# A decoder layer in split float32: cross output in two passes a pair of heads, first columns turned by VectorE and transfers

## What is computed

```python
x = x + self_attn(layernorm(x))    # blocks of 128 rows, causal softmax, one head of 512
x = x + cross_attn(layernorm(x), ctx)   # 16 heads of 32, 64 keys, silu(masked scores), no softmax
x = x + ffn(layernorm(x))          # 512 -> 2048, gelu, -> 512
```

## Time and profile before

| | us |
|---|---|
| median of 3 runs (lowest, highest) | 1262.47 (1262.35, 1262.99) |
| the profiled execution's own time | 1262.69 |
| its span | 1260.6 |
| TensorE busy | 1248.7 |
| VectorE / ScalarE / GpSimd busy | 664.6 / 487.1 / 243.5 |
| a middle step | 63.17 |

### The profile page before, as it was taken

The page is one execution under the profiler, slowest core; times in us unless marked ns, Lnnn a source line. Parts: engine busy times, 40 slices in busy tenths (PEclk is TensorE's granted clock), DMA queues, the critical chain, the costliest instruction groups (busy, mean ns, idle before and its releaser), DMA issues.

```text
span 1260.6 us, 15609 instructions
## 1 busy us (share of the span) xinstructions
PE 1248.7 (99%) x5784; PEld 1040.2 (83%) x5784; DVE 664.6 (53%) x1210; ACT 487.1 (39%) x888; POOL 243.5 (19%) x226
## 2 busy tenths in 40 slices
PE   9989999999999999999999999999999999999998
PEld 7878888888888888878888888888888888888887
DVE  7476858585858585856733333434424333434211
ACT  7246454555555555554322232222222322223221
POOL 2303232323232323258402001001001010010000
PEclk9999999999999999999999999999999999999999
DMA  8210202020202020316110020020100100100000
GB/s 296 89 63 13 76 14 75 13 76 12 75 12 75 12 75 12 125 57 211 50 67 1 1 67 1 1 67 0 57 9 0 67 0 0 67 0 0 34 1 34
DMA packets 40486, 60.04 MB, mean 48 GB/s; under 512 B 4224, under 2 KB 14464, under 8 KB 40448
## 3 DMA queue, kind: packets, MB, share of 16 engines
q1 hardware_dynamic: 40448, 59.53, 14.2%
HBM read 41.17 MB, written 18.35 MB: 47 GB/s over the span
## 4 chain that ended last, share of the span: by engine, by line
PE 55%; DVE 0%; issue 0%; DVEq 0%
PE bank L50 18%; PE bank L51 18%; PE bank L52 18%; DVE resid L1191 0%; DVEq L1190 0%
## 5 line engine op out<-in xcount | busy, mean ns | idle before, releaser
L1181 DVE TENSOR_TENSOR hid_lo<-gelu_out,hid_hi 128x512 fp32r<-128x512 f32 x128 | 98.5, 770 | 404.1 <-ACT gelu_out L1145 404.0
L50 PE MATMUL bank<-zT,w_parts 128*128 128x512 f32 x768 | 299.1, 389 | 3.4 <-DVE zT L155 1.8
L52 PE MATMUL bank<-zT,w_parts 128*128 128x512 f32 x768 | 298.8, 389 | 0.0
L51 PE MATMUL bank<-zT,w_parts 128*128 128x512 f32 x768 | 298.8, 389 | 0.0
L1141 ACT ACTIVATE hid_hi<-bank,small 128x512 fp32r<-128x512 f32 x128 | 88.3, 690 | 498.4 <-PE bank L52 498.4
L50 PE MATMUL bank<-w2p_hi,hid_lo 128*128 128x512 f32 x512 | 199.2, 389 | 0.0
L51 PE MATMUL bank<-w2p_lo,hid_hi 128*128 128x512 f32 x512 | 199.2, 389 | 0.0
L52 PE MATMUL bank<-w2p_hi,hid_hi 128*128 128x512 f32 x512 | 199.2, 389 | 0.0
L50 PEld LDWEIGHTS bank<-zT,w_parts 128*128 128x128 f32 x768 | 144.1, 188 | 34.1 <-issue 2.3
L51 PEld LDWEIGHTS bank<-zT,w_parts 128*128 128x128 f32 x768 | 144.3, 188 | 30.0
L52 PEld LDWEIGHTS bank<-zT,w_parts 128*128 128x128 f32 x768 | 144.1, 188 | 30.0
(11 more groups left out here) (142 smaller groups left out, 1805.5 us busy)
## 6 DMA issues: line engine op xcount, KB each, us to landing
x_in<-in_x SPq DMA_DIRECT2D x32, 256.0 KB, 3.1
x_dram<-resid SPq DMA_DIRECT2D x32, 256.0 KB, 2.1
w_raw<-in_w SPq DMA_DIRECT2D x32, 256.0 KB, 3.2
resid<-x_dram SPq DMA_DIRECT2D x32, 256.0 KB, 3.8
out_dram<-resid SPq DMA_DIRECT2D x32, 256.0 KB, 2.1
resid<-in_wqkvT SPq DMA_DIRECT2D x12, 256.0 KB, 4.7
mask_i<-in_mask SPq DMA_DIRECT2D x16, 128.0 KB, 2.6
values_now<-values_dram SPq DMA_DIRECT2D x8, 256.0 KB, 2.7
```

The costliest lines, as they stand in the source:

```text
L50: pe.matmul(out_ap, lhs[1], rhs[0], start=start, stop=False)
L51: pe.matmul(out_ap, lhs[0], rhs[1], start=False, stop=False)
L52: return pe.matmul(out_ap, lhs[0], rhs[0], start=False, stop=stop)
L1181: dve.tensor_tensor(hid[1][:, c % 4, :], gelu_out[:, c % 2, :], f(hid[0][:, c % 4, :]), ALU.subtract).then_inc(hid_lo, 1)
```

## The change

1. vb is one array: a pair's 64 output columns hold the values' high parts, the other 64 their low parts. A pair gets a bank of its own and two passes (with the low and the high part of attn). Half of the rows of the bank are then the high values' share and the other half the low values' share of the same output. ScalarE copies the high share of each of the chunk's two banks (64 rows each) into qo's high part, and the other half of the rows, crossed to the partner's partitions, into `rest`; VectorE subtracts (two operations of 64 rows) into o_diff; GpSimd adds o_diff and rest into qo's low part. All banks are laid out anew, and waits for them change (`outputs_out`).
2. z1 of tile a + 1 is made a step ahead: x is loaded a second time into `ahead` (four of the weight buffers), its statistics and normed rows follow a tile earlier, VectorE transposes 32 x 32 squares (4 operations of 128 x 512) into the same buffers, and 16 transfers put the squares in their places in z1_cols. ScalarE and VectorE split z1_cols instead of banks. TensorE's transposes of z1 go, but for tile 0.
3. Orders are moved: GpSimd adds the bias to x_in at the start of the step; the statistics of blocks 2 and 3 come after z2's low parts; the output shares run by halves of chunks; in the last step z3's transposes of blocks 2 and 3 stand between shares 0 and 1.

The diff, cut:

```diff
-OUT_BANK = (3, 4, 5, 1)
-BLOCK_BANK = (6, 7, 0, 2)
+PROB_BANK = 5
+SCORE_BANK = (4, 5, 6, 7, 1, 2, 7, 0)
+OUT_BANK = (7, 0, 3, 4, 0, 5, 1, 2)
+BLOCK_BANK = (3, 4, 6, 7)
+TURN_BANK = (0, 5, 1, 2)
...
+            vb = sb("vb", [P, PAIRS, P], fp32r)
+            o_diff = sb("o_diff", [P, 2, TILE])
+            o_rest = raws[:, NB:NB + 2, :]
...
-                        tuple(v[r, :, :].rearrange("p (m o) n -> p m o n", o=2)[:, :, h // 2, cols(h, HEAD_DIM)]
-                              for v in vb),
+                        tuple(vb[r, :, :].rearrange("p (m o) n -> p m o n", o=2)[:, :, h // 2, cols(at_cols, HEAD_DIM)]
+                              for at_cols in (h, (h + 2) % HEADS_PER_CHUNK)),
...
 SP
+                            if more(a):
+                                sp.wait_ge(z1_turned, NB * (a + 1))
...
+                                for r in range(QUADS):
+                                    for q in range(QUADS):
+                                        sp.dma_start(
+                                            z1_cols[cols(q, SQUARE), :, :].rearrange(
+                                                "f c (r n) -> f c r n", r=QUADS)[:, :, r, :],
+                                            raws[cols(r, SQUARE), 0:NB, :].rearrange(
+                                                "f c (q n) -> f c q n", q=QUADS)[:, :, q, :]
+                                            ).then_inc(z1_moved, 16)
+                            if twice_more(a):
+                                sp.wait_ge(z1_moved, MOVES * (a + 1))
+                                load_ahead(sp, a + 2)
...
 GpSimd
+                        def o_low(b, m, rest):
+                            pool.wait_ge(o_rested, 2 * (EC * b + m + 1))
+                            pool.wait_ge(o_diffed, 2 * (EC * b + m + 1))
+                            pool.tensor_tensor(qo[1][:, m, :], o_diff[:, m % 2, :], rest[:, m % 2, :], ALU.add
+                                               ).then_inc(o_lo, 1)
...
 ScalarE
-                            act.activation(qo[0][:, m, :], bank[banks[m]][:, :], ACT.Copy).then_inc(o_hi, 1)
+                            for n, r in enumerate(HALVES):
+                                act.activation(qo[0][r, m, :], bank[banks[2 * m + n]][r, :], ACT.Copy).then_inc(o_hi, 1)
...
+                            for n, r in enumerate(HALVES):
+                                act.activation(rest[r, m % 2, :], bank[banks[2 * m + n]][HALVES[1 - n], :], ACT.Copy
+                                               ).then_inc(o_rested, 1)
...
-                                for c in range(EC):
-                                    chunk_high(act, a, c, 4)
+                                act.wait_ge(z1_moved, MOVES * a)
+                                act.wait_ge(q_done, EC * (b + 1))
+                                z1_high(0)
+                                q_high(b, EC - 1)
+                                for c in range(1, EC):
+                                    z1_high(c)
...
                                 o_high(b, 0)
-                                o_high(b, 1)
                                 silu(b, 4)
                                 silu(b, 5)
+                                o_high(b, 1)
...
 VectorE
+                            for n, r in enumerate(HALVES):
+                                dve.wait_ge(o_hi, 2 * (EC * b + m) + n + 1)
+                                dve.tensor_tensor(o_diff[r, m % 2, :], bank[banks[2 * m + n]][r, :], f(qo[0][r, m, :]),
+                                                  ALU.subtract).then_inc(o_diffed, 1)
...
+                        def z1_low(a, c):
+                            dve.wait_ge(z1T_hi, EC * a + c + 1)
+                            dve.tensor_tensor(by_blocks(zT[1], c), by_quads(c), f(by_blocks(zT[0], c)), ALU.subtract
+                                              ).then_inc(z1T_lo, 1)
...
+                        def turn(a, blocks):
+                            if more(a):
+                                for i in blocks:
+                                    dve.transpose(turned[:, :, i, :], zn[:, i, :].rearrange(
+                                        "p (b f) -> p b f", f=SQUARE)).then_inc(z1_turned, 1)
...
+                                turn(a, range(2))
+                                mask_scores(b, 3)
+                            else:
+                                stats_ahead(dve, 1, range(NB))
+                                aggregate(dve, 1, mv1, ln1)
...
+                                low(yv, m, m, y_hi, y_lo, EC * a + m + 1)
+                                if b is None and m == 1:
+                                    rows_ahead(1, None)
...
 TensorE
-                            for n in range(2):
-                                j = 2 * m + n
-                                last = product(pe, bank[banks[m]][:, :], at(vb, j), at(attn, j % 4),
-                                               n == 0, n == 1)
+                            for j in (2 * m, 2 * m + 1):
+                                pe.matmul(bank[banks[j]][:, :], vb[:, j, :], attn[1][:, j % 4, :], start=True, stop=False)
+                                last = pe.matmul(bank[banks[j]][:, :], vb[:, j, :], attn[0][:, j % 4, :],
+                                                 start=False, stop=True)
...
+                        def outputs_out(b, m):
+                            pe.wait_ge(o_rested, 2 * (EC * b + m + 1))
+                            pe.wait_ge(o_diffed, 2 * (EC * b + m + 1))
...
-                                transposed_chunks(pe, a, 4)
...
                                 cross_output(b, 0)
-                                cross_output(b, 1)
                                 cross_scores(2)
                                 pe.wait_ge(s1_masked, NB * (a + 1))
+                                cross_output(b, 1)
+                                outputs_out(b, 0)
                                 cross_scores(3)
...
-                                    pe.wait_ge(o_lo, EC * b + i - 1)
+                                    pe.wait_ge(s2_masked, PAIRS * b + i + 3)
                                     value_rows(i)
...
                                 pe.wait_ge(s2_masked, PAIRS * (b + 1))
+                                outputs_out(b, 1)
...
+                                pe.wait_ge(keys_out, EC)
...
 TensorE, last step
+                            pe.wait_ge(q_lo, 2 * (EC * b + 4))
+                            pe.wait_ge(s2_masked, PAIRS * b + 2)
                             cross_output(b, 0, LAST_OUT_BANK)
-                            pe.wait_ge(q_lo, 2 * (EC * b + 4))
                             pe.wait_ge(s2_masked, PAIRS * b + 4)
                             cross_scores(3, LAST_SCORE_BANK)
-                            transposed_rows(pe, z3_ready, 0, 2, FIRST_BANK[2], z3T_done)
...
                             pe.wait_ge(s2_masked, PAIRS * (b + 1))
+                            for i in range(2, NB):
+                                transposed_rows(pe, z3_ready, 0, i, FIRST_BANK[i], z3T_done)
                             pe.wait_ge(o_lo, EC * b + 2)
...
                             cross_output(b, 2, LAST_OUT_BANK)
+                            pe.wait_ge(z3T_lo, 4)
                             cross_output(b, 3, LAST_OUT_BANK)
-                            transposed_rows(pe, z3_ready, 0, 3, FIRST_BANK[3], z3T_done)
```

More of the change, by code:

```diff
@@ L199, in second_residual, with squares @@
                               ).then_inc(x2_ready, 1)
+        QUADS = P // SQUARE
+        TURNS = QUADS * QUADS
+        def squares(n, to):
+            row, col = divmod(n, QUADS)
+            taken = zn[cols(row, SQUARE), :, :].rearrange("p i (c q f) -> p i c q f", c=EC, q=QUADS)
+            put = to[cols(col, SQUARE), :, :].rearrange("p c (i q t) -> p i c q t", i=NB, q=QUADS)
+            return put[:, :, :, row, :], taken[:, :, :, col, :]
         layer = ExitStack()
@@ L229, in decoder_layer_program, with by_quads, by_blocks @@
             values_stored, wo_lo = sem("values_stored"), sem("wo_lo")
-            values = [w2_raw[:, b, :] for b in range(STAGES)]
-            values.append(w1_raw[:, 0, :, :].rearrange("p c n -> p (c n)"))
+            z1_cols = sb("z1_cols", [P, EC, TILE])
+            values = [z1_cols[:, b, :] for b in range(BATCH)]
+            ahead = [raws[:, i, :] for i in range(NB)]
+            turned = raws[:, 0:NB, :].rearrange("p n e -> p (n e)").rearrange(
+                "p (c q i t) -> p (c q) i t", c=EC, q=QUADS, i=NB)
+            ahead_loaded, z1_turned = [sem(f"ahead_loaded{i}") for i in range(NB)], sem("z1_turned")
+            z1_moved = sem("z1_moved")
+            MOVES = 16 * QUADS * QUADS
+            def by_quads(c):
+                return z1_cols[:, c, :].rearrange("p (r i t) -> p i r t", r=QUADS, i=NB)
+            def by_blocks(part_, c):
+                return part_[:, c, :].rearrange("p (i r t) -> p i r t", r=QUADS, i=NB)
             RAWS = 2 * NB
```

(35 more changed lines are left out.)

226 lines of the change are left out of this document (135 added, 91 removed).

## The result

The changed kernel takes 1282.0 us (median of 4, 1281.2 to 1282.6), the kernel before 1262.6 in the runs beside it: a ratio of 1.0152, interval 1.0138 to 1.0166. Forecast were 1261.4, with a range of 1252 to 1268. TensorE's instructions went as counted, 176 fewer (5784 to 5608), and 14 us of its busy time; the span grew by 20.2 us all the same.

The account below looks back on a forecast made before the run. TensorE, busy 99% of the span, was taken to bound the kernel. Steps 0 and 1 +1.7, six middle steps -8.2 and the last step +5.4 gave -1.1 us: 1261.4 us, range 1252 to 1268.

Parts of the forecast that it names:

- the price of half-height work: Output copies and differences: half the rows save nothing, so full-height spacings, 0.48 us on ScalarE and 0.60 on VectorE.
- Up to S: Middle step to the end of the self scores: 1.79 us earlier, ending at 29.97 after the queries' start.
- Key scores 3: Middle step: waits for both output banks' copies and differences, so TensorE stands 1.7 us.
- Attention product: Middle step: starts 14.5 us after the self scores end, 0.3 late, behind probT_hi, probT_lo and mask 7.
- Fourth share: Middle step: GpSimd's addition for the fourth chunk lands at 53.8 us, exactly when needed.
- The sum: Middle step lasts 61.8 us instead of 63.17, 1.4 gained where 3.5 are removed; six such steps give -8.2.
- Steps 0 and 1: Start of the kernel: tile 1's statistics delay y's low parts, z2's transposes wait for keys_out; +1.7 us, bounds +0.8 and +3.
- Last step: Stalls of 8.3 us at outputs and shares make it end at 39.4, not 34.0: +5.4, bounds +3.5 and +7.
- B: VectorE's half-height differences cost 0.77 us each, from mask 7 to z2's last low part: 1268 us; chance 0.17.
- A: Chains shorter than drawn; half the 2.1 us stalls a step and half the last step's new 7.3 absent: 1250.4; chance 0.26.
- C: GpSimd's bias additions collide with z1's first low part, holding it up to 1.3 us in 7 steps: 1269; chance 0.08.
- D: Transfers of z1 come late and the change gives nothing; chance 0.01.

Follow-up runs that it names:

- experiments 1: Kernel before, with only the output's high copy on ScalarE and low part on VectorE each split into two 64-row operations: 1281.0 us.
- experiment 5: Kernel before, outputs 0 and 1 copied and subtracted as two 64-row x 256 pieces, outputs 2 and 3 as two 128-row x 256 pieces: 1263.1 us.
- experiment 6: Changed kernel with a chunk's four half-height copies reordered: keeping rows written in the first order 1303.8 us, keeping rows read in the second 1291.1 us.
- experiment 3: Kernel before plus only z1's turns by VectorE and transfers; three-pass cross output and last step as before: 1260.2 us.
- experiment 8: Tile 1's load issued earlier: changed kernel 1276.0 us; kernel before with z1's turns alone 1255.1; the latter with step 1's rows and turns delayed 1253.3.
- experiment 2: Changed kernel with full-height copies and one full-height difference per chunk, crossing of halves left out: 1260.9 us.
- experiment 4: Kernel before plus only the two-pass cross output, its copies and last step; z1's transposes stay on TensorE: 1294.0 us.
- the last kernel: Kernel before with z1's turns alone, tile 1's load issued earlier, and step 1's rows and turns put behind y's low parts: 1253.3 us.
- experiment 7: Changed kernel with output 0's copies put ahead of v_high 1 and its differences ahead of v_low 0: 1283.8 us.

## Why the prediction was wrong

**The step that failed** is the price of half-height work: "Those read a scalar column too, so I take the full-height spacings, 0.48 and 0.60". The number was in the trace, in the queries' halves of the earlier trace rows, and I explained it away by their scalar column. The same trace has two full-height copies with such a column, and they overlap (0.69 long, 0.59 apart):

```profile
900.77 0.69 ACT L1141 ACTIVATE hid_hi<-bank,small 128x512 fp32r<-128x512 f32 x1 [4.17 <-PE bank L52]
901.36 0.68 ACT L1145 ACTIVATE gelu_out<-bank,small 128x512 f32<-128x512 f32 x1
```

The queries' halves change their first row as well, and experiments 1, 5 and 6 show that this is what counts: 0.61 and 0.71. Here is the middle step part by part, from the end S of the self scores, 313.47. A run-out is the time in which TensorE still has its last product in the pipeline when the next should have started (0.39 long, 0.23 apart: 0.16 us).

- Up to S all held: S at T 30.0 (313.47 less 283.46) for 29.97, the turns' 1.67 gained in full (experiment 3), z1's path in time.
- Key scores 3: forecast S + 7.2, measured S + 7.5 (320.95 - 313.47), four copies of 0.61. The stall is 1.76 in the profile, forecast 1.7; with the pipeline's run-out ahead of it (0.16) 1.9.
- Attention product: forecast 0.3 late, measured 0.72, and 0.87 with the run-out; S + 15.3 for S + 14.5. Of the 8 x 0.13 on ScalarE 0.8 arrive: probT_hi ends at S + 13.9 (326.72 + 0.60 - 313.47), forecast 13.1.
- Fourth share: forecast on the dot, measured 0.69, with the run-out 0.85.
- The sum: 0.2 + 0.57 + 0.85, and three slow starts of 0.08, 1.9 us a step by this count, 1.8 by the step's length: 61.8 forecast, 63.6 measured. Seven steps have it, some 13 of the 21.6 us by which the sum was missed (-1.1 for +20.5), enough by itself to leave the range; the first steps have 5.8 beside it, the last 2.8.
- Steps 0 and 1, a second step that failed: the wait for y_lo was put too low and the clock left out. Forecast +1.7, measured +9.3, of which 1.8 is the point above. Statistics start at 50.57, the wait for y_lo is 2.92 where I had +1.2 (bounds 0.5 and 2.5). Then the clock, which stands in no term of mine: 1.7 us behind that wait (5.31 for 3.65), and as much behind the 2.02 us on zT in step 1, where the stretch from 103.48 to 107.00 has a clock of 0.54. Experiment 8 gives back 4.2 us at the queries of step 1.
- Last step: forecast +5.4, measured +8.2. The stalls were forecast as 8.3 and measure 1.57, 0.35, 2.32 and 2.96, that is 7.2, and 0.6 of run-outs: this was right. Over it lies the clock again, 0.61 and 0.72 in the two windows of 3 us behind the two long waits: eight products 0.42 apart instead of 0.23, 1.5 us each time. Not all of that is lost: in experiment 8 the last step has one such stretch, not two, and is 0.7 us shorter.

**The rivals.** B named the mechanism, and the side, with a chance of 0.17: half operations dearer than full ones. It priced VectorE's four differences at 0.77 and left ScalarE's copies at 0.48, which is where the growth of the stalls comes from; so 1268 and not 1282. A (shorter chains, 0.26) went the wrong way. C did not happen: z1's low parts last 0.69 us. What did collide is small: a mask conversion took 0.91 instead of 0.42 and the bias of the maxima 1.08 instead of 0.17, both while GpSimd worked, none on the path. These rows agree with the Trainium skill, "SBUF — State Buffer" (the part on contention), by which GpSimd and a VectorE operation in a two-port mode, or with two inputs in SBUF, exclude each other; both operations have one input, and in which mode they ran no trace shows. D is false: a transfer's issue took 0.65 us, not 0.34 to 0.51 (16 in 10.4), and still all landed long before they were wanted.

**The rule on turns.** The Trainium skill, "VectorE: DVE Perf Modes" (rules for kernel authors), sends a transpose of 128 x 128 to TensorE. Experiment 3 and two kernels of experiment 8 went the other way and gained 1.67 us a step, since TensorE is the full engine here and VectorE has room for four operations of 0.69, two on either side of a mask step. By the runs it was the turns that paid, and the two passes that lost.

**What stays open.** How much of a middle step's loss is distance and how much is that a half lasts as long as a whole was not parted by a run: experiment 2 takes away both at once, 2.8 us a step. By the rows, ScalarE's eight half copies ahead of probT_hi take 4.9 us and four full ones 1.9; of the 3.0 between them 1.0 is distance and 1.9 number, and the number was in my sum. Why a change of the first row ends the overlap is not shown, only that it does. And what decides whether the clock falls behind a wait of 1.8 us or more is open.

## What to carry to other kernels

Cost an operation by the distance to the next start in the very pattern it will have (rows, engine, neighbours), not by its duration: halves on different partitions cost a fifth to a quarter more apiece here than whole operations, and there are twice as many; halves by columns cost hardly more than the whole. Where TensorE is full, products saved are worth only what the chain that empties its banks can follow; work that leaves TensorE for an engine with room off that chain is worth its full length. And a stall of about two microseconds on TensorE may have a slower clock behind it, which took up to 1.7 us here, and nothing where TensorE had to wait again soon after.

## What the runs showed of the hardware

- Back-to-back operations of ScalarE and VectorE overlap by about 0.1 us when the first row read and the first row written stay (0.58 long, 0.48 apart; 0.68 and 0.60; also with 64 rows x 256, and from 64 rows to 128, experiment 5), and not when either changes between 0 and 64 (0.59 long, 0.61 apart; 0.69 and 0.71 in the changed kernel; one of the two kept, on ScalarE, experiment 6). The row read counts against the last operation that read PSUM, even if others stand between (0.52 against 0.64 apart, experiment 6, ScalarE).
- TensorE's granted clock fell to 1.2 GHz behind single waits of 1.84 us and more in an otherwise full stretch, but not behind each of them. It stayed at 2.4 GHz behind all waits of 1.76 or 1.77 (seven each in the changed kernel, experiment 4 and the changed kernel of experiment 8) and fell behind all seven of 1.92 (experiment 6). Behind 1.84 it fell in experiment 5 (82.59) and not in the kernel before (82.37); behind 1.89 it fell in the last kernel (83.14), and behind 1.90 at the same place of the changed kernel it didn't (87.75). Of the seven of 2.54 in experiment 6 four had it, and one of 3.04 in experiment 7 (59.16) had not. So the length of the wait alone does not decide it.
- The sixteen transfers of 64 KB, SBUF to SBUF, take 0.65 us each to issue (10.4 for all) and 2.0 to land; the stores of the earlier trace rows, 256 KB each, took 0.34 to 0.51 to issue.
